# Queries, keys and values by three 16-bit products, new orders on every engine, and products of the identity in TensorE's last list

## The reference

```python
mod = (silu(c) @ wmod).reshape(8, 6, 1, 256)        # sa, ca, ga, sb, cb, gb
h = layernorm(x) * (1 + ca) + sa
q, k, v = split(h @ w_qkv)                          # 256 x 768
q, k = elu(rope(q) * 16**-0.25) + 1, elu(rope(k) * 16**-0.25) + 1
for t in range(512):                                # for each head
    kv, ks = kv + outer(k[t], v[t]), ks + k[t]
    out[t] = (q[t] @ kv) / max(q[t] . ks, 1e-6)
x = x + ga * (out @ w_out)
h = layernorm(x) * (1 + cb) + sb
probs = softmax(h @ router_w.T)                     # 8 experts, the top 2 of each token
x = x + gb * sum_e share[e] * (gelu(h @ w1[e]) @ w2[e])
```

## Time and profile before

| | us |
|---|---|
| median of 3 runs | 785.24 |
| lowest, highest | 783.53, 786.93 |
| span of the profiled execution | 776.0 |
| attention, to the last nb | 0 to 336.4 |
| choice of experts | to 374 |
| experts | 374 to 776 |

### The profile page before, as it was taken

One profiled execution on the slowest core, in us unless ns is written; L12 is line 12 of the kernel. 1 busy time (PEld: TensorE's weight loads), 2 busy tenths in 40 slices (PEclk: granted clock), 3 DMA queues, 4 the chain that ended last, 5 costly groups with the idle time before them and its releaser, 6 DMA issues.

```text
span 776.0 us, 24871 instructions
## 1 busy us (share of the span) xinstructions
PE 714.8 (92%) x8105; PEld 549.7 (71%) x8105; DVE 628.2 (81%) x1494; ACT 571.2 (74%) x1108; POOL 518.5 (67%) x535
## 2 busy tenths in 40 slices
...
GB/s 226 113 67 133 110 135 120 131 120 139 124 140 116 151 64 67 120 48 8 96 77 69 71 73 74 76 70 79 70 75 69 77 69 76 76 72 76 72 21 1
DMA packets 52854, 69.27 MB, mean 89 GB/s; under 512 B 8864, under 2 KB 44080, under 8 KB 52736
## 3 DMA queue, kind: packets, MB, share of 16 engines
...
## 4 chain that ended last, share of the span: by engine, by line
PE 51%; DVE 2%; POOL 2%; issue 1%; DMA 1%; ACT 0%; POOLq 0%; DVEq 0%; ACTq 0%
PE hidden L1457 16%; PE bank L1475 15%; PE hidden L1459 8%; PE bank L1477 8%; PE bank L1292 2%; POOL mod_b L960 1%; PE bank L1309 0%; DMA xt<-ffn_rows,gi 0%; DMA out_dram<-x,si 0%; DVE stage L651 0%; PE bank L1300 0%; PE bank L1389 0%; POOL out_dram L1008 0%; DVE feat L652 0%; POOL mod_b L962 0%
## 5 line engine op out<-in xcount | busy, mean ns | idle before, releaser
L1457 PE MATMUL hidden<-qstT,w1hi_k 128*128 128x256 f16 x1136 | 197.9, 274 | 0.7 <-DVE qstT L755 0.7
L1459 PE MATMUL hidden<-qstT,w1lo_k 128*128 128x128 f16 x1136 | 193.6, 220 | 0.0
L1475 PE MATMUL bank<-w,amhi 128*128 x568 | 188.4, 379 | 0.1
L1477 PE MATMUL bank<-w,amlo 128*128 x568 | 154.8, 273 | 0.0
L1008 POOL DMA_INDIRECT out_dram<-x,si x71 | 115.2, 1622 | 38.8 <-issue 25.8
L791 DVE TENSOR_TENSOR amlo<-am,amhi 128x512 f16<-128x512 f32 x142 | 98.3, 693 | 49.2 <-ACT am L1168 49.2
L1457 PEld LDWEIGHTS hidden<-qstT,w1hi_k 128*128 x1136 | 111.7, 98 | 14.0 <-issue 1.1
L1459 PEld LDWEIGHTS hidden<-qstT,w1lo_k 128*128 x1136 | 111.6, 98 | 0.2
L1309 PE MATMUL bank<-wq,hT 128*128 128x512 f32 (+1 forms) x256 | 98.8, 511 | 1.3 <-DVE hT L524 1.2
L1475 PEld LDWEIGHTS bank<-w,amhi 128*128 128x128 f16 x568 | 55.6, 98 | 59.9 <-issue 0.4
L1167 ACT ACTIVATE amhi<-am 128x512 f16<-128x512 f32 x142 | 88.1, 620 | 0.3 <-DVE am L785 0.3
...
...
## 6 DMA issues: line engine op xcount, KB each, us to landing
...
```

Of the source, the lines that this page charges most:

```text
L1457: t.matmul(dst.rearrange("p (q n) -> p q n", q=2), w1s[0][k][g][:, w_], both, start=(k == 0), stop=False)
L1459: last = t.matmul(dst[:, P:2 * P], w1s[1][k][g][:, w_], both[:, 0, :], start=False, stop=(k == KT - 1))
L1475: t.matmul(y[:, :], ghi[:, m.p, c_m], w2s[mt // 2][:, bass.ds(w_, 2 * D)], start=(mt == 0), stop=False)
L1477: last = t.matmul(y[:, D:2 * D], glo[:, m.p, c_m], w2s[mt // 2][:, bass.ds(w_, D)], start=False, stop=(mt == MT - 1))
```

## The change

- From chunk 3 on (PLAIN = 3), v and qk are 16-bit: hi by hi, hi by lo and lo by hi, twelve matmuls in place of four. For that, two works are new: hh (ACT) writes the high half of the modulated transpose, hl (POOL) the low half. v and qk wait for hl. Chunks 0 to 2 go on in 32-bit.
- The weights of q, k and v are split once at the start: wqh (ACT, both high halves), wql (DVE, one low half in step 1 and one in step 2).
- shq moves from ACT to POOL. slo is one subtraction for q and k together, 512 wide, in place of two; the fourth part of each stack is set to zero once.
- mean, variance, root and offset have two buffers. rs writes over its input, and no longer waits for xn and xn2; ve does.
- hT has one buffer.
- All lists are new.
- TensorE's last list holds 22 times "fill": two products of the identity with itself, 32-bit, 128 wide, into columns of bank 4 that nobody reads.

```diff
+            def qkv_low(m):
+
+                k = m.n
+                dve.wait_ge(s_wqh, k + 1)
+                v.scalar_tensor_tensor(out=wq16[:, k, 1, :], in0=wq_raw[k], scalar=WS, in1=wq16[:, k, 0, :],
+                                       op0=ALU.mult, op1=ALU.subtract).then_inc(s_wql, 1)
...
-                g.tensor_tensor(qst[:, :, 1:4:2, :], f[:, 0].broadcast_to([P, NH, 2, HD]), qst[:, :, 0:3:2, :],
-                                ALU.subtract)
-                g.tensor_tensor(kst[:, :, 2:4, :], f[:, 1].broadcast_to([P, NH, 2, HD]), kst[:, :, 0:2, :],
-                                ALU.subtract).then_inc(a_["slo"], 1)
+                g.tensor_tensor(lows, feat[:, :].rearrange("p (q h d) -> p q h d", q=2, h=NH), highs, ALU.subtract)\
+                    .then_inc(a_["slo"], 1)
+
+            def h_low16(m):
+                if m.n < PLAIN:
+                    return
+                wait(pool, a_["hh"], m.n - PLAIN + 1)
+                g.tensor_tensor(h16[:, 1, :], hT[:, :], h16[:, 0, :], ALU.subtract).then_inc(a_["hl"], 1)
...
+            def h_high(m):
+                if m.n < PLAIN:
+                    return
+                wait(act, a_["hTe"], m.n + 1)
+                wait(act, a_["qk"], m.n)
+                wait(act, a_["v"], m.n)
+                copy(h16[:, 0, :], hT[:, :]).then_inc(a_["hh"], 1)
...
+            def product16(dst, m, lo):
+
+                for k in range(KT):
+                    hi_, lo_ = (h16[:, c, k * P:(k + 1) * P] for c in range(2))
+                    last = mm3(dst, hi_, lo_, wq16[:, k, 0, lo], wq16[:, k, 1, lo], start=(k == 0), stop=(k == KT - 1))
+                return last
...
             def v_product(m):
                 wait(pe, a_["hTe"], m.n + 1)
+                wait(pe, a_["hl"], m.n - PLAIN + 1)
...
             def steadied(m):
...
-                wait(dve, a_["rs"], m.n)
-                v.tensor_scalar(var[:, :], mv[:, :, 1], LN_EPS, None, ALU.add).then_inc(a_["ve"], 1)
+                wait(dve, a_["xn"], m.n - 1, NC)
+                wait(dve, a_["xn2"], m.n - NORM2 - 1)
+                v.tensor_scalar(rstd[:, m.p, :], mv[:, m.p, :, 1], LN_EPS, None, ALU.add).then_inc(a_["ve"], 1)
...
+            def without_reader(m):
+
+                wait(pe, a_["sth"], B * (CPB - 1))
+                wait(pe, a_["stl"], B * (CPB - 1))
+                for _ in range(2):
+                    t.matmul(bank[4][:, NH * VW:NH * VW + P], ident[:, :], ident[:, :], start=True, stop=True)
...
+    ("aT", 31), ("lg", 28), ("fill", 31), ("pj", 31), ("h2T", 29), ("fill", 31), ("fill", 31), ("fill", 31),
+    ("fill", 31), ("lg", 29), ("fill", 31), ("fill", 31), ("h2T", 30), ("fill", 31), ("fill", 31), ("fill", 31),
```

More of the change, by code:

```diff
@@ L44 @@
 VW = HD + 1
+STACK = NH * 4 * HD
 HG = 8
@@ L57 @@
 WS = 64.0
[L58 to L68, removed]
+Q_SCALE = float(HD ** -0.25)
+ORDER_PE = (("ear", 3), ("hT", 0), ("sc1", 3), ("pj", 4), ("Tk", 2), ("pv0", 3), ("h2T", 6), ("v", 0), ("Tq", 2),
+    ("lg", 6), ("pv1", 3), ("sc0", 2), ("qk", 0), ("aT", 3), ("state", 2))
@@ new lines @@
+ORDER_DVE = (("st", 0), ("den", 4), ("mv2", 5), ("mv", 0), ("rec", 4), ("stl", 4), ("ve", 0), ("at", 4), ("f", 2),
+    ("nb", 0), ("sl0", 3), ("hTe", 0), ("rope", 1), ("x1", 4), ("sl1", 3), ("wlo", 1), ("st2", 4), ("vlo", 0))
+ORDER_POOL = (("rs", 0), ("shq", 2), ("wb", 4), ("shk", 2), ("slo", 2), ("hl", 0), ("R", 1), ("xm2", 5), ("h2", 5))
+ORDER_ACT = (("exp", 2), ("sh0", 3), ("xn", 0), ("aTe", 4), ("whi", 1), ("sth", 3), ("hh", 0), ("sh1", 3),
+    ("kTs", 2), ("h2Te", 6), ("xn2", 5), ("vhi", 0), ("qTs", 2), ("lge", 6))
@@ L69 @@
+ORDER_SP = (("ldx", 0), ("modg", 6), ("modb", 7), ("so", 6), ("ro", 7), ("ld", 0), ("modgb", 6), ("gb", 6))
+OPENING_PE = {0: (("hT", 0), ("v", 0), ("qk", 0)),
+    1: (("hT", 0), ("mod1", 0), ("v", 0), ("qk", 0))}
 OPENING_DVE = {0: (("st", 0), ("mv", 0), ("ve", 0), ("nb", 0), ("hTe", 0)),
-               1: (("st", 0), ("mv", 0), ("ve", 0), ("nb", 0), ("rope", 1), ("vlo", 1), ("hTe", 0), ("wlo", 1), ("vlo", 0))}
-OPENING_ACT = {0: (("xn", 0),), 1: (("xn", 0), ("vhi", 1), ("whi", 1), ("vhi", 0))}
+    1: (("st", 0), ("mv", 0), ("ve", 0), ("nb", 0), ("vlo", 1), ("rope", 1), ("hTe", 0), ("wlo", 1), ("vlo", 0), ("wql", 1)),
+    2: (("stl", 3), ("st", 0), ("st2", 5), ("at", 3), ("wql", 1), ("mv", 0), ("ve", 0), ("sl0", 3), ("f", 2), ("nb", 0), ("den", 3), ("sl1", 3), ("x1", 4), ("rec", 3), ("hTe", 0), ("mv2", 5), ("wlo", 1), ("rope", 1), ("vlo", 0))}
@@ L72 @@
+OPENING_ACT = {0: (("xn", 0), ("hh", 0), ("wqh", 0)),
+    1: (("vhi", 1), ("hh", 0), ("whi", 1), ("xn", 0), ("vhi", 0))}
 CLOSING = 28
[L73 removed]
[11 rows of a table removed]
[L85 removed]
[13 rows of a table removed]
[L99 removed]
[5 rows of a table removed]
[L105 to L112 removed]
[4 rows of a table removed]
```

152 lines of the change are left out of this document (99 added, 53 removed), and 65 rows, old and new, of tables (CLOSING_ACT, CLOSING_DVE, CLOSING_PE, CLOSING_POOL).

## The result

The changed kernel takes 792.12 us in the median (791.72 to 798.31, 5 runs), the kernel before 785.56 beside it (783.53 to 786.93, 5 runs): ratio 1.0096, 95% interval 1.0063 to 1.013. The forecast was 775.5 in a range of 765 to 785 and 71% for faster. It is slower by 1%, outside the range.

A forecast was written before the change was run, and what follows sets the result against it. A ring of waits through PE, DVE and POOL set the 9.46 us attention step; DVE's list would then give 9.2. Loop -7, opening +2, closing -4.4 sum to -9.4 from 785.24: 775.5, range 765 to 785.

The forecast's parts named there:

- joints: DVE's steady list: other work now separates instructions that needed the one just before; 0.3 us a step saved (0 to 0.5).
- (a): DVE from ve to nb, round POOL's rs: at and f cover it, so no new wait; 0.35 a step if rs is 1.07.
- (b): DVE from nb to hTe, round ACT's xn and PE's hT: only sl0 covers it, new wait 0.2 (0 to 0.4).
- (c): ACT's hh stands ahead of sh1, so DVE waits 0.4 in three steps of four: 0.3 a step (0 to 0.45).
- (d): DVE's f might be held while POOL's rs reads its operands: taken as 0; 0.55 us a step by the skill's rule.
- Opening: First chunks: DVE gains two low halves of the weight, 1.9 us together; +2 in all.
- Closing: End of the attention loop: fills keep PE at 2.4 GHz (-3.5), with -0.3 and -0.6 for the rest; -4.4 us.
- The constant: Whole run: the 785.24 median lies 9.2 us above the 776.0 profiled span, for what lies around; carried over unchanged.
- Rival 2: DVE's order takes back in (b) and (c) all it saves; step stays 9.4, time 783; chance 0.14.
- Rival 5: POOL's hl comes late, so PE's v and the next step shift; 9.9 us a step, 795; chance 0.08.
- Rival 3: PE's clock falls in spite of the fills: +6 after pj31, the 3.5 not won; 785; chance 0.06.
- Rival 4: DVE's f waits for POOL's rs to be through; step 9.75, time 791; chance 0.05.

The follow-up runs named there:

- a_nofills: The changed kernel without its 22 fills on TensorE; ratio 1.0070 to the kernel before.
- w_nohh: a_wait without hh on ACT: DVE's hTe writes the high half, hl subtracts that from itself (output not the reference's); ratio 0.9879 to the kernel before.
- a_wait: The changed kernel with one wait added: in the steady loop POOL's xm2 also waits for ACT's vhi; 778.70 against 783.35 before, ratio 0.9951.
- b_fills: The kernel before with 22 fills added to TensorE's last list; 778.63 against 779.47, ratio 0.9989.
- b16_fills: The 16-bit product under the old orders, with hh and hl put in, and the 22 fills; 804.01, ratio 1.0325 to the kernel before.

## Why the prediction was wrong

**The failed step: DVE's list.** The sum was 9.0 - 0.3 + 0.2 + 0.3 = 9.2 us; 9.92 came, in the slowest run, and 9.67 in the trace of a_nofills. So the loop, put at -7 us, cost 3 (a_nofills) to 9. The sum priced a hold of wlo at nothing, and that was 0.27 to 0.37 a step. DVE's busy time between 60 and 260 us, in one step: 9.12 before (191.31 of 200, times 9.53), 9.16 after (184.59 of 200, times 9.92). Of the latter 0.37 is the hold (a half lasts 0.91 and 0.82 on average in the two kinds, in place of 0.68), so its own work is 8.79. Term by term:
- joints: -0.3 forecast, -0.33 found.
- (a) ve to nb: 0 and 0. rs lasts 0.70 in all 20 steps looked at, as taken.
- (b) hTe behind hT: 0.2 forecast, 0.40 found (8.0 us in 20 steps), the upper bound.
- (c) sl1 behind hh: 0.3 forecast, 0.16 found, and shown by w_nohh.
- (d) f beside rs: 0 and 0 (f 0.68 at 166.55, with rs running since 166.26).
- the hold of wlo by xm2: 0.37, absent from the sum. I kept 0.69 for an instruction whose neighbour on POOL the change moved.
- the small waits left: 0.21, set to nothing because I started from the busy time and not from the step. In this trace they are mostly the dips of the clock, 0.23 in all; the clock was taken as 1.00 up to the last lg.
- the base: 9.46 is the commonest step before and 9.53 the mean, so DVE's 9.0 should have been 9.1.

So waits and the hold are 1.14 a step, where waits were 0.41 before, and that more than used up what a shorter list and a shorter ring had set free. Without holds and dips, as in a_wait, the step is 9.34: the list's own terms were short by 0.14.

I weighed the Trainium skill's rule on shared ports at one place only, f beside rs, found a row against it, and closed the case. rs reads two numbers a partition; xm2 reads 256. The row was right and said nothing of xm2. The rule bites at wlo, where two instructions that both last near 0.7 start 0.01 us apart.

**PE.** v and qk are twelve 16-bit matmuls, 1.97 us a step (192.68 to 193.34 and 195.61 to 196.92 in the changed kernel; 1.94 forecast). That this is worth up to 0.83 was the bound; it is worth about 0.1.

**Opening.** +2 forecast, +5 found (39.5 in a_nofills, 34.5 in b_fills). The weight's halves are some 2.7 of it. Not seen: in ACT's list of step 1 xn stands behind an instruction that waits for a DMA, 2 to 4 us. The list showed it; I priced only what ACT and DVE had to do, not what stood ahead of what.

**Closing.** -4.4 forecast; the clock was kept and gave 0.9 of the 3.5. Against the trace before, on chips of one speed, nb27 to nb36 is 1.9 shorter in a_nofills and the part behind it 1.1: 3.0 us without any fill, which is the new orders' work. There half clock, on an engine that the others outlast, cost 0.9 us in 12; in the loop, where DVE waits for pj, 3.4 us of it cost 1.3.

**The constant.** The 9.2 us between the median and the profiled span are not what lies around a run: each run of the changed kernel is 1.7 to 2.0 above its own span (798.31 and 796.5). By the last column of the table the rest is the chip of that trace. It stood on both sides of the sum and did no harm.

**The rivals.** Rival 2 (step 9.4) was nearest in kind. Rival 5 had the right time (795) for the wrong reason: no wait for hl shows in the changed kernel, though b16_fills is just this. Rival 3's clock did not fall where the fills stand; it fell in the loop, which no rival had. Rival 4 named the right mechanism at the wrong pair. The chances don't quite add up: rivals 4 and 5 are 0.13, and what lies within 0.16.
